# Quantised self-attention on Trainium2: chunk-bias products in 128x64 tiles, and another order of work on all engines

## The reference

```python
def _chunk_decompose(x2d):          # chunks of 32 rows
    ch_bias = (jnp.max(xp, axis=1, keepdims=True) + jnp.min(xp, axis=1, keepdims=True)) / 2
    xz = xp - ch_bias
    tmax = jnp.max(jnp.abs(xz), axis=(1, 2))
    cmax = jnp.max(jnp.abs(xz), axis=1)
    thr = tmax[:, None] / 2.0 ** jnp.arange(DECOMP - 1, -1, -1, dtype=jnp.float32)
    idx = jnp.sum(cmax[:, :, None] > thr[:, None, :DECOMP - 1], axis=-1)
    scale = tmax[:, None] / 2.0 ** (DECOMP - 1 - idx).astype(jnp.float32) / Q_MAX
    result = _sym_qdq(xz, scale[:, None, :])
...
def proj(w_orig, w_dq_t, b):
    y = result @ w_dq_t + ch_bias @ w_orig.astype(jnp.float32).T
    return y.reshape(-1, H)[:n] + b
...
attn = jnp.einsum('bqhd,bkhd->bhqk', Q, K)
probs = jax.nn.softmax(attn, axis=-1)
ctx = jnp.einsum('bhqk,bkhd->bqhd', probs, V).reshape(bsz * tgt, H)
r2, cb2, n2 = _chunk_decompose(ctx)
out = (r2 @ WO + cb2 @ o_weight.astype(jnp.float32).T).reshape(-1, H)[:n2] + o_bias
```

## Time and profile before

| | |
|---|---|
| median of 3 runs | 3126.77 us (3124.7 to 3126.9) |
| the profiled execution | 3125.24 us |
| its span | 3123.2 us |
| busy share of PE, DVE, ACT, POOL | 89%, 64%, 42%, 40% |
| mean granted clock of PE | 0.943 |

### The profile page before, as it was taken

How to read it: one execution, slowest core, us unless ns; L and a number is a source line. 1 busy time by engine, 2 the same in 40 slices (tenths; PEclk the granted TensorE clock), 3 DMA queues, 4 the chain that set the end, 5 groups by cost and what they waited for, 6 DMA issues and landing times. The chain is left out here.

```text
span 3123.2 us, 64555 instructions
## 1 busy us (share of the span) xinstructions
PE 2777.4 (89%) x23444; PEld 2366.0 (76%) x23444; DVE 2001.9 (64%) x4027; ACT 1327.3 (42%) x3154; POOL 1262.0 (40%) x1605
## 2 busy tenths in 40 slices
PE   6999999985999999999999699967999999599993
PEld 6888888874888888888888588855777777377772
DVE  5555555554788888888888444434767767366656
ACT  2222222223666665666656422212333334266656
POOL 3111111112666676767666211112444444234334
PEclk9999999997999999999999899987888888799997
DMA  3000000002000000000000100010000000100001
GB/s 133 7 7 7 4 6 7 7 0 91 6 3 5 5 3 5 3 5 3 5 3 3 41 0 0 0 32 11 8 11 7 7 10 0 37 25 27 24 11 58
DMA packets 42647, 49.10 MB, mean 16 GB/s; under 512 B 4176, under 2 KB 33744, under 8 KB 42064
## 3 DMA queue, kind: packets, MB, share of 16 engines
q1 hardware_dynamic: 42576, 48.16, 4.7%
HBM read 35.57 MB, written 4.19 MB: 13 GB/s over the span
## 5 line engine op out<-in xcount | busy, mean ns | idle before, releaser
L1019 ACT ACTIVATE b_probs<-bank,b_shift,b_q_scale 128x128 f32<-128x128 f32 x512 | 227.8, 458 | 71.1 <-DVE b_shift L896 71.1
L1078 POOL TENSOR_TENSOR b_rows<-b_rows,b_swapped 128x512 f32<-128x512 f32 x160 | 204.0, 1283 | 133.5 <-DVE b_swapped L865 133.5
L46 PE MATMUL bank<-a_xT,a_wq 128*128 128x256 f32 x512 | 150.6, 294 | 49.5 <-DVE a_xT L371 49.5
L505 POOL TENSOR_TENSOR a_probs<-a_probs,a_rs 128x512 f32<-128x512 f32 x64 | 66.8, 1043 | 306.3 <-DVE a_rs L404 299.1
L1125 POOL TENSOR_TENSOR b_probs<-b_probs,b_rs 128x512 f32<-128x512 f32 x128 | 133.1, 1040 | 112.6 <-DVE b_rs L916 109.2
L1088 POOL TENSOR_TENSOR b_rms<-b_rms,sh_minus_half 128x8 f32<-128x8 f32 (+1 forms) x128 | 169.6, 1325 | 10.7
L873 DVE TENSOR_REDUCE b_ss<-b_squares 128x4 f32<-128x512 f32 x192 | 125.2, 680 | 60.7 <-ACT b_squares L994 60.7
L124 POOL TENSOR_SCALAR sh_rstd<-sh_meanvar 128x2 f32<-128x2 f32 (+1 forms) x80 | 17.8, 222 | 344.4 <-DVE sh_meanvar L116 265.2
L46 PE MATMUL bank<-b_wo,b_oT 128*128 128x256 f32 x512 | 150.6, 294 | 1.4 <-DVE b_oT L839 1.4
L46 PE MATMUL bank<-a_wo,a_oT 128*128 128x256 f32 x512 | 147.0, 287 | 0.0
L48 PE MATMUL bank<-b_wo,b_oT 128*128 128x256 f32 x512 | 145.6, 284 | 0.0
(11 more groups left out here) (350 smaller groups left out, 9217.5 us busy)
## 6 DMA issues: line engine op xcount, KB each, us to landing
a_xT_in<-in_xT SPq DMA_DIRECT2D x16, 256.0 KB, 2.6
sh_x<-in_x SPq DMA_DIRECT2D x1, 4096.0 KB, 24.9
b_ctx_in<-in_ctxT SPq DMA_DIRECT2D x32, 128.0 KB, 2.0
d_x_in<-sh_x SPq DMA_DIRECT2D x16, 256.0 KB, 2.3
e_x_in<-sh_x SPq DMA_DIRECT2D x16, 256.0 KB, 2.3
e_cT<-in_ctxT SPq DMA_DIRECT2D x32, 128.0 KB, 2.5
out<-sh_x SPq DMA_DIRECT2D x16, 256.0 KB, 2.1
a_qT<-in_L_attn_Wq SPq DMA_DIRECT2D x1, 2048.0 KB, 8.4
```

The lines of the kernel that those rows point to most:

```text
L46: pe.matmul(out, left[0], right[0], start=start, stop=False)
L1019: op = act.activation(probs[:, g % 2, keys], bS[:, keys], ACT.Exp, bias=shift[:, g % 2, a:a + 1], scale=q_scale[:, g, a // 2, a % 2:a % 2 ...
L1078: pool.tensor_tensor(rows[:, unit, :], rows[:, unit, :], swapped[:, half, :], ALU.add).then_inc(added[unit], 1)
```

## The change

The eight bias products of `spread_x` are each done in two of 64 output channels, with weights of 128x64 in place of 128x128. The order of `turn` changes on PE, DVE, ACT and POOL. `moments` is called for `oldest` at the head of DVE's turn in place of `old` at its end; `maximum` of units 0 and 1, `shift` and `exponent` of unit 0, `exponent` of unit 1, `take_v`, `take_pT` of unit 0 and `project_v(…, 0)` move from the end of one turn to the next; `weigh(4)`, `turn_probs(7)`, `exponent(6)`, `exponent(7)`, `take_pT(6)` and `take_pT(7)` also move to the next turn, where their group is `old`. On POOL `compare(qc)` comes ahead of `spread_bias` and `add_out_bias`.

```diff
--- before.py
+++ after.py
@@ -2216,8 +2216,10 @@
                     for o in range(C):
                         at = YB.start + (m * C + o) * M
                         for c in range(C):
-                            op = pe.matmul(bX[1][:, at:at + M], w[:, m, c, o * 128:(o + 1) * 128], qx.bias[:, c * M:(c + 1) * M],
-                                           start=(c == 0), stop=(c == C - 1))
+                            for side in range(2):
+                                op = pe.matmul(bX[1][side * 64:(side + 1) * 64, at:at + M],
+                                               w[:, m, c, o * 128 + side * 64:o * 128 + (side + 1) * 64], qx.bias[:, c * M:(c + 1) * M],
+                                               start=(c == 0), stop=(c == C - 1))
                 op.then_inc(qx.top_spread, 1)
 
             def spread_att(i):
@@ -2328,27 +2330,30 @@
                 op.then_inc(weighed[u], 1)
 
             def turn(new, mid, old, oldest):
+                project_v(mid, 0)
+                turn_x(new, oldest)
                 scores(mid, 0, 0, 5, True)
-                weigh(old, 7)
-                turn_x(new, oldest)
+                scores(mid, 0, 1, 7, True)
+                weigh(old, 4)
+                turn_probs(old, 7, 6, False)
                 project_v(mid, 1)
                 weigh(old, 6)
-                scores(mid, 0, 1, 7, True)
+                weigh(old, 7)
+                turn_probs(mid, 0, 7, True)
                 scores(mid, 1, 0, 1, False)
-                turn_probs(mid, 0, 7, True)
                 turn_att(old, mid)
+                turn_probs(mid, 1, 0, False)
+                scores(mid, 1, 1, 2, False)
                 weigh(mid, 0)
-                turn_probs(mid, 1, 0, False)
-                scores(mid, 1, 1, 3, False)
                 turn_probs(mid, 2, 1, False)
                 weigh(mid, 1)
-                weigh(mid, 2)
                 turn_cmax(new, qx, bX[1], qc, old, v_taken[1])
                 turn_probs(mid, 3, 2, False)
                 spread_x(new)
+                weigh(mid, 3)
                 turn_probs(mid, 4, 3, False)
                 turn_cmax(old, qc, bX[0], qx, new, res_ready)
-                weigh(mid, 3)
+                weigh(mid, 2)
                 turn_probs(mid, 5, 4, False)
                 spread_att(old)
                 weigh(mid, 5)
@@ -2356,12 +2361,9 @@
                 project_k(new, old, 0)
                 project_k(new, old, 1)
                 project_q(new, 0)
-                weigh(mid, 4)
                 project_q(new, 1)
-                turn_probs(mid, 7, 6, False)
                 project_out(old, new, 0)
                 project_out(old, new, 1)
-                project_v(new, 0)
 
             pe.wait_ge(w_ready, 4)
             pe.wait_ge(out_bias_ready, 1)
@@ -2533,49 +2535,49 @@
                     dve.bn_aggr(sh.meanvar[:, r, :], sh.stats[:, r, :]).then_inc(meanvar_ready, 1)
 
             def turn(new, mid, old, oldest):
+                moments(oldest)
+                lowest(new, qx, bX[0])
+                maximum(mid, 0)
+                highest(new, qx, bX[0])
+                shift(mid, 0)
+                maximum(mid, 3)
+                maximum(mid, 1)
                 shift(mid, 1)
-                lowest(new, qx, bX[0])
-                highest(new, qx, bX[0])
-                take_att(old, 1, 6)
                 maximum(mid, 2)
-                maximum(mid, 3)
+                shift(mid, 3)
+                take_att(old, 1, 7)
                 shift(mid, 2)
-                widest(new, qx)
-                shift(mid, 3)
+                maximum(mid, 5)
                 lowest(old, qc, bX[1])
                 highest(old, qc, bX[1])
-                centre(new, qx, bX[0])
+                widest(new, qx)
                 maximum(mid, 4)
                 centre(old, qc, bX[1])
                 shift(mid, 4)
                 find_top(new, qx, bX[1])
-                maximum(mid, 5)
+                centre(new, qx, bX[0])
                 widest(old, qc)
                 shift(mid, 5)
                 thresholds(new, qx, bX[1])
+                maximum(mid, 7)
                 maximum(mid, 6)
-                maximum(mid, 7)
-                shift(mid, 6)
-                count(new, qx)
                 add_bias(new)
                 find_top(old, qc, bX[0])
-                take_att(mid, 0, 3)
+                count(new, qx)
+                shift(mid, 6)
+                take_att(mid, 0, 2)
                 invert(new, qx)
                 thresholds(old, qc, bX[0])
                 divide(new, qx)
                 restore(new, qx, v_ready)
                 count(old, qc)
-                shift(mid, 7)
                 invert(old, qc)
                 divide(old, qc)
                 restore(old, qc, y_ready)
                 take_k(new)
+                shift(mid, 7)
                 take_q(new)
                 residual(old)
-                moments(old)
-                maximum(new, 0)
-                maximum(new, 1)
-                shift(new, 0)
 
             four_deep(dve, n_turns, turn)
 
@@ -2610,24 +2612,24 @@
                 act.copy(pT[:, u % 4, :, :], bP[:, :].rearrange("p (j n) -> p j n", j=4)).then_inc(pT_taken[u], 1)
 
             def turn(new, mid, old, oldest):
+                exponent(old, 6)
+                exponent(old, 7)
+                take_pT(old, 6)
+                exponent(mid, 0)
+                take_pT(old, 7)
+                take_v(mid, 0)
+                take_v(mid, 1)
+                exponent(mid, 1)
+                take_pT(mid, 0)
+                take_pT(mid, 1)
                 exponent(mid, 2)
-                take_pT(mid, 1)
                 exponent(mid, 3)
                 take_pT(mid, 2)
+                take_pT(mid, 3)
                 exponent(mid, 4)
-                take_pT(mid, 3)
                 exponent(mid, 5)
                 take_pT(mid, 4)
-                exponent(mid, 6)
                 take_pT(mid, 5)
-                take_pT(mid, 6)
-                exponent(mid, 7)
-                take_pT(mid, 7)
-                take_v(new, 0)
-                exponent(new, 0)
-                exponent(new, 1)
-                take_v(new, 1)
-                take_pT(new, 0)
 
             four_deep(act, n_turns, turn)
 
@@ -2708,20 +2710,20 @@
                                    ALU.add).then_inc(xb_ready, 1)
 
             def turn(new, mid, old, oldest):
+                compare(oldest, qc)
                 find_scale(oldest, qc)
-                spread_bias(mid, qx, v_ready)
+                spread_bias(oldest, qc, y_ready)
                 spread_k(mid)
+                add_out_bias(old)
+                find_bias(new, qx)
+                find_spans(new, qx)
                 if oldest is not None:
                     normalise(pool, sh, oldest.n, 2, meanvar_ready, norm_step, norm_done)
-                find_bias(new, qx)
-                find_spans(new, qx)
                 find_bias(old, qc)
+                spread_bias(new, qx, v_ready)
                 find_spans(old, qc)
                 compare(new, qx)
                 find_scale(new, qx)
-                add_out_bias(old)
-                spread_bias(old, qc, y_ready)
-                compare(old, qc)
 
             four_deep(pool, n_turns, turn)
```

## The result

The changed kernel takes 3076.03 us (median of 4 runs, 3073.93 to 3077.75) against 3126.84 us for the kernel before on the same chip: ratio 0.9839, 95% interval 0.9822 to 0.9856.

What follows compares the result with a forecast made beforehand. PE (89% busy) bounds the kernel, partly at a low clock. Turns of 30.75 us for 33.38 save 34 us over 13, other turns 4, drain loses 1: 37 off 3125.24 gives 3088, plus 1.5, so 3089, range 3080 to 3118.

Steps and rivals of the forecast that it cites:

- the low stretch: Low PE clock falling in every steady turn 1.8 us after spread_x's end, for 6.8 us; turn settles at 30.75 us.
- a turn with no fall at all: Sign of a wrong forecast: the clock never falls in a turn, making the kernel faster than the range 3080 to 3118.
- Part 1, the tiles: spread_x in 64-column tiles: 32 matmuls at 36 ns, 1.16 us, saving 0.69 us; bounds nothing and 0.8 us.
- Part 2, PE's order: PE's moved work at full clock: 12.6 us to last scores, 4.37 to spread_x's end, 7.0 from project_k to project_out's end.
- is worth nothing on the path: restore(old) coming earlier gains nothing, since project_out has PE's work before it in either case.
- Part 3, ACT: PE's 0.51 us idle before turn_att goes, leaving 12.1 us; 0 to 0.5 may return before turn_probs(mid, 1), 0 taken.
- Part 5, POOL: From spread_x's end (E) to project_k's start (K): kept at 6.0 us, bounds 5.5 and 6.8, though POOL's copies move away.
- a chain sets it, not PE: From spread_x's end to project_k's start, 6.07 to 6.18 us in all four turns, set by thresholds, maxima, divide, restore.
- The sum without low time: Steady turn without low clock behind project_k's start: 12.1 + 4.37 + 6.0 + 7.0 = 29.47 us, against 31.3.
- The first: Rival: sum 0.5 to 0.7 us too low; two short stretches alternate with one long, 31.9 us a turn, 3106; 27%.
- Better than the sum: Rival: spread_x's end to project_k's start 5.5 us or less, or less idle; turn not much below 30.5; 3080 to 3084; 5%.
- The late weigh(2): Rival: weigh(mid, 2) ends late, delaying DVE's chain; project_k starts 7.2 us after spread_x's end, 34.1 us turns, 3135; 8%.

Runs made afterwards that it cites:

- tiles_alone: Kernel before with only spread_x in 128x64 tiles, every order as it was: 3112.65 us, ratio 0.9958 to the kernel before.
- order_alone: Changed kernel with spread_x in 128x128 weights again, keeping the new orders: 3098.41 us, ratio 0.9914 to the kernel before.
- early_thresholds_gap: Changed kernel with DVE's thresholds(old) ahead of take_att(mid, 0, 2) and invert(new), plus two unread 256-column products before weigh(mid, 5): 3063.51 us, ratio 0.9805.
- pool_order_alone: Kernel before with only POOL's turn order of the changed kernel: 3116.43 us, ratio 0.9975 to the kernel before.
- tiles_and_pool_order: Kernel before with the 64-column tiles and POOL's new order, PE, DVE and ACT orders as before: 3086.78 us, ratio 0.9883.
- weigh2_back: Changed kernel with weigh(mid, 2) ahead of turn_cmax(new) again, as before: 3084.10 us, ratio 0.9868 to the kernel before.
- early_thresholds: Changed kernel with DVE's thresholds(old) moved ahead of take_att(mid, 0, 2) and invert(new): 3080.33 us, ratio 0.9867 to the kernel before.
- two_fillers: Changed kernel with one unread 256-column product ahead of the transposes in each of turn_probs(4) and turn_probs(5): 3075.78 us, ratio 0.9841 to the kernel before.

## Why the prediction was right in sign and wrong in size

**Where the difference lies.** The profiled execution took 3073.93 us where the sum gave 3088. Against the prediction's 30.75 us a turn, the steady turns make 0.6 us x 13 = 8 us of this. By that alone the time would be 3081, just inside the range. Load and drain saved 6.6 us where it had 3, which is 3.6 more: the start gained 8.4 us, above all in the first turn, and the end lost 1.8. Why the first turns gained so much was not tested. Some 2.6 us lie outside this block, where the two kernels are the same.

**The step that failed** is the one on the low stretch: "PE's work behind the last scores is still short work, so I expect the fall in every turn", with a stretch of 6.8 us that begins 1.8 us after E. It took the new spread_x as the same kind of short work as the old one, only shorter. tiles_alone shows that this half of the change removes the early fall from all 13 turns, and order_alone that without it the early fall is always there. In the changed kernel 4 turns of 13 have no fall and 7 a late one of 3.4 us, and the mean turn is 30.15 us. Whether the new spread_x acts through its shorter time or through the shape of its tiles was not separated. The prediction did name "a turn with no fall at all" as what would make it faster than its range, and gave 5% to all that would be better than its sum; none of its rivals let the clock stay up or fall later.

**Part 1, the tiles.** 1.05 us measured, 1.16 taken from the row of weighing: 33 ns an instruction, so fewer moving columns saved a little, as the bound of 0.8 us had it. The Trainium skill's rule in "TensorE: Matmul & The Clock Gate", section "LDWEIGHTS (loading the stationary operand)", that the load goes by its columns alone, would have left 1.85 us; here it does not hold for pairs of half-width tiles, and the measurement decides.

**Part 2, PE's order.** 12.25 us up to the last scores (12.1 forecast), 4.10 to E (4.37; 0.11 of the difference is the tiles, the rest idle time of PE, 5.06 less 4.89 us in the earlier trace rows, that is gone). K to the end was forecast at 7.0 us and is 8.10 without low clock. A second, smaller step failed here, the one in part 5: restore(old) earlier "is worth nothing on the path". With k and q projected at full clock PE reaches project_out before qc.result and k_taken are there, and waits 0.86 us for take_k, which stands behind restore(old) on DVE. early_thresholds_gap, without that wait, has 7.11 us: the term itself was right, the wait was missing.

**Part 3, ACT.** The idle before turn_att went; 0.41 us came back before turn_probs(1), where the text had said that there was no margin and took 0.

**Part 5, POOL.** E to K is 5.39 us. The text had 5.5 as a bound, from qc's own divide and restore, and kept 6.0 since it expected cold work of PE. In order_alone, with the early fall, it is 5.75 to 6.74: the choice followed from the failed step. The opening of the prediction has "a chain sets it, not PE" for all four turns of the earlier trace rows. In the last of them PE is busy 6.03 of the 6.18 us, and in pool_order_alone such turns still take 6.17 us with a shorter chain, so PE's cold work sets K as well there. The edit of POOL is shown to be the cause by pool_order_alone.

**The sum without low time** was 29.47 us and is 29.85: 1.1 us too little for the wait, 0.6 and 0.3 too much for E to K and the tiles. Up to the last scores 0.15 was missing. It was near for reasons that cancel. That a turn settles into a repeating one with the same stretch each time was seen, in tiles_and_pool_order (30.72 us), weigh2_back (30.72) and early_thresholds (30.66), but not in the changed kernel, which goes through a cycle of six turns.

**The rivals.** None of them occurred in the changed kernel as it was described. The first came true in order_alone, where the tiles save nothing. "Better than the sum" had the right E to K of 5.5 us or less but kept the fall, with 30.5 us as the least turn. The late weigh(2) did not occur: in the whole block DVE waited 0.9 us in all for a weighing before the reciprocals of take_att, in the changed kernel and in order_alone. Where the fall comes early, K is at 5.7 us in the changed kernel and up to 6.7 in order_alone, and PE has no idle time before project_k: its own cold work is what is late.

## What to carry to other kernels

When a clock that can fall bounds a stage, price not only the work that an edit removes but what it leaves PE doing around the place where the clock falls: here a faster group of narrow products removed the early fall, and a few wide products in an idle gap removed the late ones. Ask then where the fall moves to: here one over the wide projections cost half its length, and one over a wait little or nothing. A wait and a low clock can hide each other, so removing either alone shows no gain (early_thresholds, two_fillers), and both together do.

## What the runs showed of the hardware

- Two 128x64 tiles of float32 weights, one for each half of the output partitions, took 33 ns an instruction where a 128x128 tile took 116: 32 instructions in 1.05 us against 16 in 1.85.
- Added products of 216 to 256 columns in four places (wide_filler) put the fall of the clock late in 8 turns of 13. About the same time of PE in products of 8 columns in the same places (narrow_filler) left it near E in all 13.
- Six more transposes, inside PE's idle time (two_transpose_fillers), took the turns without a fall from 4 to 10 of 13 and left no late one; E to K stayed at 5.4 us in them. The Trainium skill's page "TensorE: Matmul & The Clock Gate", section "Part 4: PE-mode transpose", has it that transposes don't count as activity of PE in the way products do. For these, which the trace lists as matmuls with the identity, this case does not agree.
- POOL's addition and copy of 128x512 beside DVE's divide and restore made these 0.5 and 0.2 us longer: 1.21 and 0.98 us before, 0.69 and 0.75 in pool_order_alone.
